# A routed expert layer on one core: two weighing pieces in front of the weights, two buffers of turned lists, a residual apart from its statistics, and last norms on VectorE

## Chip, core and metric

The kernel runs on 1 core of one Trainium2 chip. The metric is the device time of the whole program in microseconds; the median of three runs stands for a kernel.

## What is computed

Input x is 4 sequences of 1024 tokens with 128 features. The first half is a gated recurrence along the tokens, then a residual and a layer norm. The second half, on which the change works, sends every token to experts by product keys:

```python
xn = batch_norm(x)
q = (xn @ w_q.T).reshape(b, n, 2, h, kd).transpose(2, 0, 1, 3, 4)    # h = 8 heads
sim = einsum('pbnhd,hkpd->pbnhk', q, keys)                           # 32 keys a side
s, i = top_k(sim, 8)
all_scores = sx[..., :, None] + sy[..., None, :]
scores, pk = top_k(all_scores.reshape(b, n, h, 64), 8)
idx = take(ix * 32 + iy, pk)                                         # of 1024 experts
o = gelu(einsum('bnd,bnhkd->bnhk', x, key_in[idx])) * softmax(scores)
y = einsum('bnhk,bnhkd->bnd', o, key_out[idx])
out = layernorm(x + y)
```

## The kernel before

The tokens are worked in `NS = 16` steps m of 256 tokens; two steps make a chunk q of 512 (`NCH = 8`). The experts are not gathered. All 1024 inner products with `key_in` are made (`experts_in`, then `gelus`), the 64 chosen weights of each token are spread into a dense table p (`scatter`), the two tables are multiplied (`weigh`), and the product goes through `key_out` (`experts_out`).

Each engine has its own written order, and semaphores tie the orders together. For a step m the work passes:

- PE `scores`, ScalarE `sims_out`, VectorE `greatest` (8 largest of 32, L651) and `indices` (L659).
- GpSimd `candidate_sums` (last operation L265), ScalarE `exps` and `low_halves`, VectorE `top_sums` (L665).
- GpSimd `candidate_codes` (L270 to L281) and `over_eighth` (L287), ScalarE `signs` (L434).
- In the next step, VectorE `pack` (L672), `pick` (L684), then `sums_and_codes`: a copy of `exk` (L691), `codes` from `picked` and `masks` (L692), a sum and a reciprocal. GpSimd's `weights` (L292 to L301) and ScalarE's `convert` write `lists`. PE turns the lists, ScalarE copies them out of PSUM into `listsT` (`lists_out`, L444), and VectorE `hots_of` makes one-hot tables of each half of the lists (L708, L714, L718, twice in a step).
- PE `scatter` multiplies the one-hot tables, ScalarE `p_out` (L453) copies p into `pn`, and GpSimd `weigh` (L308) multiplies four pieces of 512 elements for each partition, `gl = pn * gl`, two steps later still.

GpSimd's order in a step m is `candidate_sums(m)`, `weights(m-1)`, `weigh(m-3)`, `candidate_codes(m)`, `over_eighth(m)`. VectorE's order is `greatest(m)`, `pack`, `pick` and `sums_and_codes` of m-1, `indices(m)`, `top_sums(m)`, `hots_of(m-1, 0)`, in odd steps from 5 on a `residual` with its `stats`, and `hots_of(m-1, 1)`. ScalarE runs `gelus` in steps 1, 2, 3, 5, 7, 9, 11 and 13, and `signs(m)` stands inside them, in front of the third piece.

The tail is written out by hand. Step 14's second half and step 15 go through `quarters` on PE, which keeps the two parts of each weight apart; ScalarE takes the low part (L531), and VectorE adds the high part and weighs (`both_parts`, L818 and L823). GpSimd weighs the first half of step 14 (L325). The last chunk is normed in two halves of 256 tokens.

Of the kernel before, what the change touches and what calls it, by code (L numbers as in the profile page):

```python
# [5 lines left out]
ALU = mybir.AluOpType  # L6
ACT = mybir.ActivationFunctionType
AX_X = mybir.AxisListType.X
F32 = mybir.dt.float32
F16 = mybir.dt.float16  # L10
# [4 lines left out]
P = 128  # L15
# [10 lines left out]
def seqffn_kernel(nc, x, w_in, w_select, w_gate, w_out, w_delta, log_a, gamma, beta, w_q, keys,  # L26
# [8 lines left out]
    NCH = T // CH  # L35
# [6 lines left out]
    NS = T // 2  # L42
# [11 lines left out]
    with ExitStack() as ctx:  # L54
        def sb(name, shape, dt=F32):
            return ctx.enter_context(nc.sbuf_tensor(name, shape, dt))
# [60 lines left out]
        masks = sb("masks", [P, 2, 1], U16)  # L117
        codes = sb("codes", [P, 2, 2 * SL], U16)
        lists = sb("lists", [P, 4, 2 * SL], F16)
        listsT = sb("listsT", [P, 2, 4, P // 2], F16)  # L120


        XW, YW = P * NI // 2, P * NJ // 2
# [9 lines left out]
        zf = nat[:, 0:CH, :]  # L133
        st2 = sb("st2", [P, CH, 6])
        mv2 = sb("mv2", [P, CH, 2])
        rstd2 = sb("rstd2", [P, CH])
# [49 lines left out]
        def wait(eng, name, value):  # L186
            if value <= 0:
                return
            eng.wait_ge(s[name], value)
# [33 lines left out]
        def _(pool):  # L223
# [27 lines left out]
            def candidate_sums(m):  # L251
                wait(pool, "vals_done", m * 2 + 2)
                wait(pool, "top_done", m)
                wait(pool, "dt_done", m)
                vx, vy = vals[:, 0], vals[:, 1]
                pool.tensor_tensor(cand[:, :, 0:8], vx[:, :, 0:1].to_broadcast([P, RH, 8]), vy, ALU.add)  # L256
                pool.tensor_tensor(cand[:, :, 8:12], vx[:, :, 1:2].to_broadcast([P, RH, 4]), vy[:, :, 0:4], ALU.add)
                pool.tensor_tensor(cand[:, :, 12:16].rearrange("p h (a b) -> p h a b", a=2),
                                   vx[:, :, 2:4].unsqueeze(3).to_broadcast([P, RH, 2, 2]),
                                   vy[:, :, 0:2].unsqueeze(2).to_broadcast([P, RH, 2, 2]), ALU.add)  # L260
                pool.tensor_tensor(cand[:, :, 16:20], vx[:, :, 4:8], vy[:, :, 0:1].to_broadcast([P, RH, 4]),
                                   ALU.add).then_inc(s["cand_done"], 1)
                wait(pool, "cand_done", m + 1)
                wait(pool, "ex_done", m)
                pool.tensor_tensor(dif[:, :, :], cand[:, :, :], cand[:, :, 0:1].to_broadcast([P, RH, NCAND]),  # L265
                                   ALU.subtract).then_inc(s["dif_done"], 1)
# [33 lines left out]
                wait(pool, "whi_done", m + 1)  # L300
                pool.tensor_tensor(lists[:, 3, :], flat, lists[:, 2, :], ALU.subtract).then_inc(s["wlo_done"], 1)  # L301

            def weigh(m):
                wait(pool, "p_evac", m * 2 + 2)
                wait(pool, "gelu_done", (m // 2 + 1) * JR)
                for r in range(4):
                    js = slice(4 * r, 4 * r + 4)
                    pool.tensor_tensor(gl[:, m % GL, js], pn[:, m % 3, js], gl[:, m % GL, js],  # L308
                                       ALU.mult).then_inc(s["a_done"], 1)

            for m in range(NS):
                candidate_sums(m)
                if m >= 1:
                    weights(m - 1)
                if m >= 3:
                    weigh(m - 3)
                candidate_codes(m)
                over_eighth(m)
            weigh(NS - 3)
            pool.wait_ge(s["hot_done"], 2 * NS)  # L320
            pool.wait_ge(s["p_evac"], LAST)
            for r in range(4):
                js = slice(4 * r, 4 * r + 4)
# [5 lines left out]
        def _(act):  # L329
# [110 lines left out]

            def lists_out(m):
                wait(act, "lists_mm", m + 1)
                wait(act, "hot_done", m * 2)
                act.activation(listsT[:, :, :, :].rearrange("p h f t -> p f h t"),  # L444
                               b_lists.rearrange("p (f h t) -> p f h t", f=4, h=2), ACT.Copy).then_inc(s["lists_evac"], 1)

            def p_out(m, hf):
# [31 lines left out]
            def spread2_half(u):  # L479
# [1 line left out]
                act.wait_ge(s["mv2_done"], NCH + u)  # L481
                act.wait_ge(s["out_done"], NCH - 1)
                act.activation(rstd2[:, n], mv2[:, n, 1], ACT.Sqrt, bias=eps[:, 0:1]).then_inc(s["sd2"], 1)

            def norm_out_half(u):
                act.wait_ge(s["nmr2_done"], NCH + u)
                act.wait_ge(s["stored"], 16 * (NCH - 1))
                for t in range(2 * u, 2 * u + 2):
                    end = act.activation(outb[:, t, :], zf[:, t, :], ACT.Identity, bias=nmr2[:, t:t + 1],
                                         scale=rstd2[:, t:t + 1])  # L490
                end.then_inc(s["out_done"], 1)

            normed(0)
            sims_out(0)
# [40 lines left out]
            norm_out(NCH - 2)  # L535
            for u in range(2):
                spread2_half(u)
                norm_out_half(u)

        @block.vector  # L540
        def _(dve):
# [158 lines left out]
            def hots_of(m, hf):  # L700
                at = slice(32 * hf, 32 * hf + 32)

                def spread(f, n):
                    v = listsT[:, hf, f, :].rearrange("p (g s) -> p g s", s=2)
                    return v.unsqueeze(2).to_broadcast([P, 32, n, 2])

                wait(dve, "lists_evac", m + 1)
                dve.tensor_tensor(hoty[:, at], iota[:, NI:].unsqueeze(1).to_broadcast([P, 32, NJ, 2]),  # L708
                                  spread(1, NJ), ALU.is_equal).then_inc(s["hoty_done"], 1)
                if m * 2 + hf == 2 * NS - 1:  # L710
                    dve.wait_ge(s["q_mm"], 2)
                else:
                    wait(dve, "p_mm", m * 2 - 1 + hf)
                dve.tensor_tensor(hotx[:, at], iota[:, 0:NI].unsqueeze(1).to_broadcast([P, 32, NI, 2]),  # L714
                                  spread(0, NI), ALU.is_equal)
                wait(dve, "hoty_done", m * 2 + hf + 1)
                both = listsT[:, hf, 2:4, :].rearrange("p w (g s) -> p (w g) s", s=2).unsqueeze(2)
                dve.tensor_tensor(hotw[:, :, at].rearrange("p w g j s -> p w (g j s)"),  # L718
                                  hoty[:, at].rearrange("p g j s -> p (g j s)").unsqueeze(1).to_broadcast(
                                      [P, 2, 32 * NJ * 2]),  # L720
                                  both.to_broadcast([P, 64, NJ, 2]), ALU.mult).then_inc(s["hot_done"], 1)
# [79 lines left out]
                    end = dve.bn_aggr(mv2[:, t, :], st2[:, t, :])  # L801
                end.then_inc(s["mv2_done"], 1)

            def last_scales(u):
                n = slice(2 * u, 2 * u + 2)
                dve.wait_ge(s["sd2"], NCH + u)
                dve.reciprocal(rstd2[:, n], rstd2[:, n]).then_inc(s["rstd2_done"], 1)
                dve.wait_ge(s["rstd2_done"], NCH + u)
                dve.scalar_tensor_tensor(out=nmr2[:, n], in0=mv2[:, n, 0], scalar=-1.0, in1=rstd2[:, n],
                                         op0=ALU.mult, op1=ALU.mult).then_inc(s["nmr2_done"], 1)  # L810

            def both_parts(h):
                m, hf = (LAST + h) // 2, (LAST + h) % 2
# [12 lines left out]
            dve.wait_ge(s["gelu_done"], NCH * JR)  # L826
            both_parts(0)
            residual(NCH - 2)
            stats(NCH - 2)
            both_parts(1)  # L830
            both_parts(2)
            scales(NCH - 2)
            for u in range(2):
                last_residual(u)
                last_scales(u)

        @block.tensor
        def _(pe):
# [215 lines left out]
```

## Time and profile before

| what | value |
|---|---|
| median of 3 runs | 490.32 us (487.49 to 490.91) |
| profiled execution, its own time | 490.44 us |
| its span, first to last instruction | 488.5 us |
| mean granted TensorE clock | 0.787 of full speed |
| busy: PE, VectorE, ScalarE, GpSimd | 359.3, 432.3, 245.4, 243.5 us |
| steps 1 to 15 begin on VectorE | 93 us to 428 us |
| last instruction of step 15's hot tables | ends 468.0 us |

Busy time of an engine is the union of its instructions' time. An idle time in square brackets stands before an instruction, with the engine and line that ended it. An instruction that waits inside the engine for a memory port shows no idle time: it shows a longer duration. So the durations of one line have to be compared over its repetitions.

### The profile page before, as it was taken

The page shows a single profiled execution, that of the slowest core. Times are in us where ns is not written, and L with a number is a line of the kernel's source. Part 1 is how long each engine was busy: PE and PEld are TensorE (multiplying, and loading weights), DVE is VectorE, ACT ScalarE, POOL GpSimd, SP SyncE. Part 2 cuts the span into 40 slices and gives each one's busy share as a digit, 9 for nine tenths or more (in the row PEclk, how much of TensorE's full clock was granted, in tenths as well). Part 3 has the DMA queues.
Part 4 walks back from the last instruction along what each step waited for, and adds up shares of the span by engine and source line. Part 5 has one row for each costly group of instructions (what it writes and reads, how often), then busy time and mean ns, then how long its engine had stood idle before and what let it go on. Part 6 is the DMA issues. An engine that isn't in the chain of part 4 may idle for free.

```text
span 488.5 us, 23430 instructions
## 1 busy us (share of the span) xinstructions
PE 359.3 (74%) x9713; PEld 266.5 (55%) x9713; DVE 432.3 (88%) x2701; ACT 245.4 (50%) x402; POOL 243.5 (50%) x341
## 2 busy tenths in 40 slices
PE   5979858137877778778777887687688778687565
PEld 3445544015545466447655674467356747487555
DVE  2458986999999869999999999989999999999993
ACT  2897664354555534364556445545464456242233
POOL 1023350453529461828382969262929483969030
PEclk9979956767595977797599768877797598867579
DMA  8900000000000000000000000000000000000001
GB/s 241 192 3 1 1 1 0 1 1 3 4 2 5 3 3 4 5 2 5 25 5 3 3 26 3 5 3 26 3 4 4 25 5 3 4 26 4 3 25 44
DMA packets 7658, 8.90 MB, mean 18 GB/s; under 512 B 896, under 2 KB 6912, under 8 KB 7424
## 3 DMA queue, kind: packets, MB, share of 16 engines
q1 hardware_dynamic: 6976, 7.34, 5.8%
q8 instruction: 76, 1.25, 1.1%
q14 instruction: 30, 0.25, 0.2%
q10 hardware_dynamic: 576, 0.07, 0.1%
HBM read 5.31 MB, written 2.10 MB: 15 GB/s over the span
## 4 chain that ended last, share of the span: by engine, by line
DVE 37%; PE 29%; issue 12%; POOL 5%; ACT 3%; DVEq 0%; ACTq 0%; POOLq 0%
PE psum L993 10%; DVE idx L659 7%; PE psum L946 7%; PE psum L980 6%; DVE vals L651 5%; DVE picked L684 5%; DVE arena L718 5%; DVE arena L714 4%; PE psum L926 4%; DVE arena L708 3%; POOL arena L308 2%; DVE top L665 2%; PE psum L918 1%; DVE words L672 1%; POOL code L278 1%
## 5 line engine op out<-in xcount | busy, mean ns | idle before, releaser
L946 PE MATMUL psum<-arena 64*64 64x16 f16 x7424 | 88.3, 182 | 61.0 <-issue 55.3
L946 PEld LDWEIGHTS psum<-arena 64*64 64x64 f16 x7424 | 81.2, 120 | 79.1 <-issue 73.6
L993 PE MATMUL psum<-ko,arena 64*128 64x128 f32 x1024 | 92.2, 358 | 1.9 <-issue 1.9
L993 PEld LDWEIGHTS psum<-ko,arena 64*128 64x128 f32 x1024 | 88.8, 269 | 2.9 <-issue 2.5
L659 DVE FIND_INDEX8 idx<-vals,sims 128x8 uint32<-128x32 f32 x512 | 82.6, 186 | 0.0
L714 DVE TENSOR_TENSOR arena<-iota,listsT 128x4096 f16<-128x4096 f16 x32 | 75.5, 2359 | 0.0
L980 PE MATMUL psum<-x1T,trn 128*64 128x256 f32 x512 | 65.6, 410 | 13.1 <-ACT arena L461 12.4
L308 POOL TENSOR_TENSOR arena<-arena 128x512 f32<-128x512 f32 x56 | 69.6, 1276 | 0.0
L980 PEld LDWEIGHTS psum<-x1T,trn 128*64 128x64 f32 x512 | 35.1, 146 | 49.7 <-ACT arena L461 25.4
L256 POOL TENSOR_TENSOR cand<-vals 128x128 f32<-128x128 f32 x16 | 9.4, 587 | 104.5 <-DVE vals L651 104.5
L453 ACT ACTIVATE arena<-psum 128x1024 f32<-128x1024 f32 x29 | 29.5, 1017 | 60.8 <-PE psum L946 60.8
L651 DVE MAX8 vals<-sims 128x8 f32<-128x32 f32 x512 | 49.0, 173 | 3.4 <-ACT sims L413 3.4
L926 PE MATMUL psum<-msim,xn 128*128 128x512 f32 x64 | 47.0, 875 | 1.2 <-ACT xn L405 1.2
L684 DVE MAX8 picked<-words 128x8 f32<-128x20 f32 x512 | 43.2, 164 | 5.0 <-ACT words L429 3.2
L461 ACT ACTIVATE arena<-psum 128x512 f32<-128x512 f32 x64 | 37.0, 595 | 13.3 <-PE psum L980 13.2
L718 DVE TENSOR_TENSOR arena<-arena,listsT 128x2048 f16<-128x2048 f16 x32 | 41.2, 1288 | 0.0
L659 DVE MATCH_VALUE_LOAD idx<-vals,sims 128x8 f32 x512 | 36.6, 72 | 0.0
L708 DVE TENSOR_TENSOR arena<-iota,listsT 128x1024 f16<-128x1024 f16 x32 | 26.1, 816 | 8.2 <-ACT listsT L444 8.2
L240 POOL TENSOR_TENSOR arena<-arena 128x512 f32<-128x512 f32 x8 | 10.3, 1286 | 45.4 <-ACT arena L370 45.4
L413 ACT ACTIVATE sims<-psum 128x512 f32<-128x512 f32 x32 | 19.0, 596 | 21.5 <-PE psum L926 21.2
L444 ACT ACTIVATE listsT<-psum 128x512 f16<-128x512 f16 x16 | 9.6, 597 | 37.4 <-PE psum L933 32.3
L862 PE MATMUL psum<-arena,trn 128*128 128x512 f32 x48 | 24.6, 652 | 1.7 <-ACT arena L373 1.7
(126 smaller groups left out, 570.2 us busy)
## 6 DMA issues: line engine op xcount, KB each, us to landing
x<-in_L_attn_x_dram SPq DMA_DIRECT2D x8, 256.0 KB, 5.6
out_dram<-nat SPq DMA_DIRECT2D x7, 256.0 KB, 2.5
ko<-in_L_ffn_key_out_dram SPq DMA_DIRECT2D x2, 512.0 KB, 9.9
nat<-in_L_ffn_key_in_dram SPq DMA_DIRECT2D x2, 256.0 KB, 10.1
nat<-in_L_ffn_keys_dram SPq DMA_DIRECT2D x2, 128.0 KB, 5.5
out_dram<-nat SPq DMA_DIRECT2D x2, 128.0 KB, 1.7
nat<-in_L_attn_W_delta_dram SPq DMA_DIRECT2D x1, 64.0 KB, 2.8
nat<-in_L_attn_W_in_dram SPq DMA_DIRECT2D x1, 64.0 KB, 2.7
```

Source lines behind the costliest of these rows:

```text
L308: pool.tensor_tensor(gl[:, m % GL, js], pn[:, m % 3, js], gl[:, m % GL, js], ALU.mult).then_inc(s["a_done"], 1)
L461: act.activation(gl[:, (2 * q) % GL:(2 * q) % GL + 2, 2 * r:2 * r + 2, :].rearrange("p m j w -> p j m w"), b_g[r % 2].rearrange("p (j m w) ...
L651: end = dve.max(vals[:, p, t * H + h, :], sims[:, m % 2, t, r, :])
L659: end = dve.max_index(idx[:, p, t * H + h, :], vals[:, p, t * H + h, :], sims[:, m % 2, t, r, :])
L684: end = dve.max(picked[:, w, r, :], words[:, w, r, :])
L708: dve.tensor_tensor(hoty[:, at], iota[:, NI:].unsqueeze(1).to_broadcast([P, 32, NJ, 2]), spread(1, NJ), ALU.is_equal).then_inc(s["hoty_don ...
L714: dve.tensor_tensor(hotx[:, at], iota[:, 0:NI].unsqueeze(1).to_broadcast([P, 32, NI, 2]), spread(0, NI), ALU.is_equal)
L718: dve.tensor_tensor(hotw[:, :, at].rearrange("p w g j s -> p w (g j s)"), hoty[:, at].rearrange("p g j s -> p (g j s)").unsqueeze(1).to_br ...
L926: pe.matmul(b_sim[t], xn[:, t], msim[:, :], start=True, stop=True).then_inc(s["sim_mm"], 1)
L946: end = pe.matmul(psum[64 * e:64 * e + 64, at:at + NJ], hotx[rows, g, :, e], hotw[rows, part, g, :, e], start=(part == 0), stop=(part == 1))
L980: end = pe.matmul(b_g[r % 2][64 * e:64 * e + 64, b * SW:(b + 1) * SW], trn[:, 9 + r, 64 * b:64 * b + 64], tokens[:, e], start=True, stop=True)
L993: end = pe.matmul(y2[:, e, m % 2] if m < NS - 1 else y_last[:, e], gl[rows, m % GL, j, :], ko[rows, j, :], start=(j == 0), stop=(j == NJ - 1))
```

## The change

- GpSimd: `weigh` takes a range of pieces. Pieces 0 and 1 of `weigh(m-3)` move ahead of `weights(m-1)`; pieces 2 and 3 stay behind it.
- `listsT` gets two buffers by the parity of m; `lists_out(m)` waits for the hot tables of step m-2 where it waited for those of m-1.
- GpSimd's last weighing (L325) waits for 31 of the 32 hot tables where it waited for all.
- Tail on VectorE: `residual` of chunk 6 (steps 12 and 13) stays ahead of `both_parts(1)`, and its `stats` move behind it.
- The last two half norms move from ScalarE (two activations with bias and scale) to VectorE (two subtract-and-multiply operations), and the small operation that made their bias goes.

```diff
+        listsT = sb("listsT", [P, 2, 2, 4, P // 2], F16)
...
+            def weigh(m, first=0, last=4):
                 wait(pool, "p_evac", m * 2 + 2)
                 wait(pool, "gelu_done", (m // 2 + 1) * JR)
+                for r in range(first, last):
...
             for m in range(NS):
                 candidate_sums(m)
+                if m >= 3:
+                    weigh(m - 3, 0, 2)
                 if m >= 1:
                     weights(m - 1)
                 if m >= 3:
-                    weigh(m - 3)
+                    weigh(m - 3, 2, 4)
                 candidate_codes(m)
                 over_eighth(m)
             weigh(NS - 3)
-            pool.wait_ge(s["hot_done"], 2 * NS)
+            pool.wait_ge(s["hot_done"], 2 * NS - 1)
...
             def lists_out(m):
                 wait(act, "lists_mm", m + 1)
-                wait(act, "hot_done", m * 2)
-                act.activation(listsT[:, :, :, :].rearrange("p h f t -> p f h t"),
+                wait(act, "hot_done", m * 2 - 2)
+                act.activation(listsT[:, m % 2].rearrange("p h f t -> p f h t"),
...
             for u in range(2):
                 spread2_half(u)
-                norm_out_half(u)
...
-            def last_scales(u):
+            def last_out(u):
                 n = slice(2 * u, 2 * u + 2)
                 dve.wait_ge(s["sd2"], NCH + u)
                 dve.reciprocal(rstd2[:, n], rstd2[:, n]).then_inc(s["rstd2_done"], 1)
                 dve.wait_ge(s["rstd2_done"], NCH + u)
-                dve.scalar_tensor_tensor(out=nmr2[:, n], in0=mv2[:, n, 0], scalar=-1.0, in1=rstd2[:, n],
-                                         op0=ALU.mult, op1=ALU.mult).then_inc(s["nmr2_done"], 1)
+                dve.wait_ge(s["stored"], 16 * (NCH - 1))
+                for t in range(2 * u, 2 * u + 2):
+                    end = dve.tensor_scalar(outb[:, t, :], zf[:, t, :], mv2[:, t:t + 1, 0], rstd2[:, t:t + 1],
+                                            ALU.subtract, ALU.mult)
+                end.then_inc(s["out_done"], 1)
...
             both_parts(0)
             residual(NCH - 2)
+            both_parts(1)
             stats(NCH - 2)
-            both_parts(1)
             both_parts(2)
             scales(NCH - 2)
             for u in range(2):
                 last_residual(u)
-                last_scales(u)
+                last_out(u)
```

## Rows read from the trace of the kernel before

**Rows 1.** The page's part 1: busy us, share of the span, instructions of each engine.

```profile
PE 359.3 (74%) x9713; PEld 266.5 (55%) x9713; DVE 432.3 (88%) x2701; ACT 245.4 (50%) x402; POOL 243.5 (50%) x341
```

**Rows 2.** The page's part 4: the chain that ended last, by engine.

```profile
DVE 37%; PE 29%; issue 12%; POOL 5%; ACT 3%; DVEq 0%; ACTq 0%; POOLq 0%
```

**Rows 3.** Timeline of GpSimd, step 8: start us, us, line, operation.

```profile
266.46 0.72 POOL L265 TENSOR_TENSOR dif<-cand 128x320 f32<-128x320 f32 x1
269.40 0.25 POOL L292 TENSOR_SCALAR zscaled<-zinv 128x16 f32<-128x16 f32 x1 [2.22 <-DVE zinv L698]
...
271.03 4.96 POOL L308 TENSOR_TENSOR arena<-arena 128x512 f32<-128x512 f32 x4
275.93 0.76 POOL L270 CAST iyf<-idx 128x128 f32<-128x128 uint32 x1
...
284.70 0.75 POOL L287 TENSOR_TENSOR above<-cand,top 128x320 f32<-128x320 f32 x1
```

**Rows 4.** Timeline of VectorE, the same step 8.

```profile
268.20 0.31 DVE L691 COPY exk<-picked 128x256 uint16<-128x256 uint16 x1
268.41 0.42 DVE L692 TENSOR_TENSOR codes<-picked,masks 128x256 uint16<-128x256 uint16 x1
...
275.61 0.93 DVE L708 TENSOR_TENSOR arena<-iota,listsT 128x1024 f16<-128x1024 f16 x1
```

**Rows 5.** Timeline after step 15: GpSimd's weigh of step 13, VectorE beside it.

```profile
447.93 5.19 POOL L308 TENSOR_TENSOR arena<-arena 128x512 f32<-128x512 f32 x4
...
448.56 1.03 DVE L672 SCALAR_TENSOR_TENSOR words<-sgn,code 128x320 uint16<-128x320 f32 x1 [0.56 <-issue]
...
452.50 0.78 DVE L691 COPY exk<-picked 128x256 uint16<-128x256 uint16 x1
```

**Rows 6.** One line's instructions: duration ns min/median/max, first and last start us.

```profile
L672 DVE SCALAR_TENSOR_TENSOR words<-sgn,code x16: 492/497/1034, 96.1 to 448.6; 128x320 uint16<-128x320 f32 x16
...
L708 DVE TENSOR_TENSOR arena<-iota,listsT x32: 658/754/1248, 106.9 to 464.0; 128x1024 f16<-128x1024 f16 x32
```

**Rows 7.** Timeline, step 1: GpSimd's L287 between two hot tables of VectorE.

```profile
110.09 1.73 POOL L287 TENSOR_TENSOR above<-cand,top 128x320 f32<-128x320 f32 x1
...
111.13 1.23 DVE L708 TENSOR_TENSOR arena<-iota,listsT 128x1024 f16<-128x1024 f16 x1
```

**Rows 8.** VectorE idle: timeline of steps 4 and 10, then the waits (us, times, longest).

```profile
167.86 1.39 DVE L684 MAX8 picked<-words 128x8 f32<-128x20 f32 x16 [1.89 <-ACT words L429]
180.88 0.69 DVE L708 TENSOR_TENSOR arena<-iota,listsT 128x1024 f16<-128x1024 f16 x1 [4.00 <-ACT listsT L444]
...
324.39 0.69 DVE L708 TENSOR_TENSOR arena<-iota,listsT 128x1024 f16<-128x1024 f16 x1 [2.02 <-ACT listsT L444]
...
DVE arena L708 <- ACT listsT L444: 8.2, 5, 4.0
DVE picked L684 <- ACT words L429: 3.2, 3, 1.9
```

**Rows 9.** Timeline of ScalarE, step 3, inside the gelus.

```profile
161.99 0.47 ACT L434 ACTIVATE sgn<-above 128x320 f32<-128x320 f32 x1 [0.86 <-POOL above L287]
```

**Rows 10.** Timeline of the tail, VectorE, GpSimd and PE.

```profile
459.73 0.69 DVE L708 TENSOR_TENSOR arena<-iota,listsT 128x1024 f16<-128x1024 f16 x1 [0.72 <-ACT listsT L444]
...
468.06 3.75 POOL L325 TENSOR_TENSOR arena<-arena 128x256 f32<-128x256 f32 x4 [14.94 <-DVE arena L718]
...
471.18 0.87 DVE L733 BATCH_NORM_STATS2 st<-nat 128x6 f32<-128x128 f32 x4
472.09 0.38 DVE L737 BATCH_NORM_AGGREGATE mv<-st 128x2 f32<-128x6 f32 x4
...
473.10 1.04 PE L970 MATMUL psum<-arena 64*64 64x32 f16 x64 [2.57 <-DVE arena L818]
```

**Rows 11.** Timeline: a norm on VectorE in the first half, the last norm on ScalarE.

```profile
67.04 2.14 DVE L617 TENSOR_SCALAR x<-x,mv,rstd 128x128 f32<-128x128 f32 x8
...
485.52 0.88 ACT L489 ACTIVATE nat<-nat,nmr,rstd 128x128 f32<-128x128 f32 x2 [0.43 <-DVE nmr L809]
```

More of the change, by code:

```diff
@@ L119, in seqffn_kernel @@
         lists = sb("lists", [P, 4, 2 * SL], F16)
-        listsT = sb("listsT", [P, 2, 4, P // 2], F16)
+        listsT = sb("listsT", [P, 2, 2, 4, P // 2], F16)
         XW, YW = P * NI // 2, P * NJ // 2
@@ L301, in weights @@
                 pool.tensor_tensor(lists[:, 3, :], flat, lists[:, 2, :], ALU.subtract).then_inc(s["wlo_done"], 1)
-            def weigh(m):
+            def weigh(m, first=0, last=4):
                 wait(pool, "p_evac", m * 2 + 2)
                 wait(pool, "gelu_done", (m // 2 + 1) * JR)
-                for r in range(4):
+                for r in range(first, last):
                     js = slice(4 * r, 4 * r + 4)
@@ L483, in spread2_half @@
                 act.activation(rstd2[:, n], mv2[:, n, 1], ACT.Sqrt, bias=eps[:, 0:1]).then_inc(s["sd2"], 1)
[L485 to L491, printed above, removed]
             normed(0)
@@ L703, in spread @@
                 def spread(f, n):
-                    v = listsT[:, hf, f, :].rearrange("p (g s) -> p g s", s=2)
+                    v = listsT[:, m % 2, hf, f, :].rearrange("p (g s) -> p g s", s=2)
                     return v.unsqueeze(2).to_broadcast([P, 32, n, 2])
@@ L716, in hots_of @@
                 wait(dve, "hoty_done", m * 2 + hf + 1)
-                both = listsT[:, hf, 2:4, :].rearrange("p w (g s) -> p (w g) s", s=2).unsqueeze(2)
+                both = listsT[:, m % 2, hf, 2:4, :].rearrange("p w (g s) -> p (w g) s", s=2).unsqueeze(2)
                 dve.tensor_tensor(hotw[:, :, at].rearrange("p w g j s -> p w (g j s)"),
```

## The prediction

> **What bounds the kernel now.** I read the busy shares first: VectorE is busy for 432.3 of 488.5 us, and no other engine for more than 74% [rows 1]. The chain of waits says the same less sharply, with VectorE at 37%, PE at 29% and GpSimd at 5% [rows 2]. Then I took VectorE's idle times by what ended them. Between steps 1 and 15 there are few: 8.2 us ahead of the hot tables (L708), 0.72 of it in the tail, and 3.2 us in the middle of `pick` (L684) [rows 8, 10]. So in the steps VectorE sets the pace, and PE is the second limit: where L708 waits 4.00 us in step 4 and 2.02 us in step 10, the lists were ready and PE came to turn them late. Whatever makes VectorE's own instructions longer is paid in nearly every step; whatever makes GpSimd faster is paid back only where somebody waits for it.
>
> The next thing to read is not idle time but duration. VectorE and GpSimd hold each other up inside their instructions. L672 takes 0.49 us in the steps and 1.03 us once, at 448.56, while GpSimd weighs; L691, elsewhere 0.31 us, takes 0.78 us at 452.50, and ends just after the fourth weighing piece [rows 4 to 6]. In step 1 GpSimd's L287 waits for a hot table to end and then holds the next, L708, to 1.23 us against its 0.68: 0.55 us for an instruction that takes 0.75 undisturbed [rows 3, 6, 7]. The two engines take turns: a GpSimd instruction that asks while a VectorE one holds goes next, ahead of VectorE's following one.
>
> **Two pieces ahead of the weights, steps 3 to 15.** Step 8 stands for all. GpSimd ends L265 at 267.18 and then idles 2.22 us until the reciprocal is there at 269.4 [rows 3]. Two pieces of 4.96 / 4 = 1.24 us fit almost: 267.13 to 269.6. On GpSimd that delays the weights by 0.2 us at most, and the turned lists came in front of their use by over 1 us in such steps, so that costs nothing. It starts the codes as soon as the indices are done, 1.3 us ahead of the hot tables and 1.6 us earlier than now.
>
> But in those 2.22 us VectorE runs L691 (from 268.20) and L692 (from 268.41) [rows 4]. Today GpSimd is idle there and four pieces run beside the index searches, which show no delay. After the change piece 0 lets go at about 268.3: L691 loses 0.0 to 0.1. Piece 1 is ready at 268.35, before L692 starts, and takes its turn when L691 lets go, at about 268.5. L692 then waits for the whole piece. No row shows L692 beside GpSimd, nor a whole 512-element piece ahead of a VectorE instruction, so this is bounded. Below: 0, if L692 gets in first or does not mind; then piece 1 runs on beside the index searches. Above: L287 held for its 0.75 less 0.2 us, so a piece holds for 1.24 less 0.2, or 1.05. By elements, 0.55 x 512 / 320 = 0.88. Below zero is excluded, since nothing of VectorE's is removed there. I take 1.05: L692 reads two tiles in SBUF like L708 and L672, which both were held, and the order of requests favours the piece.
>
> The Trainium skill, "SBUF — State Buffer", section "Who interferes with whom", speaks against this edit: an instruction of VectorE with two SBUF inputs and one of GpSimd that reads SBUF exclude each other for the whole instruction, in order of issue. Rows 5 and 7 agree, with 0.54 and 0.55 us. "GPSIMD Engine Reference", section "Instruction dispatch", puts two inputs at 2.5 cycles an element; at its 1.2 GHz that would be an estimate of 1.07 us a piece, and the sum would be the same within 0.2 us.
>
> How often is it paid? In ten steps in full (3, 5, 7 to 11, 13 to 15). In step 4 the wait in `pick` of 1.89 us [rows 8] moves L691 behind both pieces: nothing. In steps 6 and 12 smaller waits of the same kind leave about 0.35 each. Sum 10 x 1.05 + 0.7 = 11.2 us. Some of it falls into idle time that VectorE has anyway, since PE came late there: 1.05 of step 3 in the 5.9 us of step 4; 2.0 of steps 9 and 10 in the 2.02 of step 10; and steps 6 and 12 share the rest of the two waits (8.2 - 4.0 - 2.0 - 0.7 and 3.2 - 1.9, or 2.8 us), which takes 1.4 of steps 5 and 6 and 0.8 of steps 11 and 12 [rows 8]. Absorbed 5.2, left +6.0 us.
>
> **What the earlier codes give.** In step 8 the tail of weighing no longer holds L708 (0.93 against 0.68, so 0.25 [rows 4, 6]), and three code instructions fewer take turns at 0.09 each: 0.5 gained. But `over_eighth` (L287), which now ends behind the hot tables at 285.4 [rows 3], falls between them as in step 1, at 0.55. Net 0, from -0.1 to +0.1 a step. L287 is earlier by some 4 us, and ScalarE's signs with it. VectorE does not wait for the signs in the steps. They hold up the gelus only 0.86 us in step 3 [rows 9], and by as much in steps 7 and 13, where VectorE has no idle time after them to give back. Step 3's gives -0.9, through PE, in step 4.
>
> **The tail.** (a) `weigh(13)` starts earlier and meets L718 and L672 where it met L672 and L691; against that L672's idle 0.56 goes [rows 5]. L718 and L672 lose about 1.0 and 0.8, before 0.53, 0.47 and 0.56: with L287's 0.55, net +0.4, taken between -0.5 and +1.5. (b) With two buffers `lists_out(15)` no longer waits for the hot tables of step 14, and L708's 0.72 goes [rows 10]; next is VectorE itself, so -0.7. In the steps this buffer changes nothing. (c) L325's four pieces, 3.75 us with one VectorE instruction of 1.2 in between, hence 0.63 each holding 0.44, now begin beside `scales` and the last hot table and hold up four VectorE instructions: up to 4 x 0.44; I take +1.4. Its results were not awaited before 474, so earlier is no gain. (d) The chain ends over L818 of `both_parts(1)`, for which PE waits 2.57 us, then 9.3 us of `experts_out`. Statistics of 0.87 + 0.38 go behind it: -1.25. What is late next is `both_parts(2)`, which stays where it was and was ahead of the second `experts_out` by just about this, so the gain may end at 1.0. (e) The last norm: 0.88 us and a hop on ScalarE plus 0.16 for the bias become two instructions at 2.14 / 8 = 0.27 on VectorE [rows 11], about 0.45 less. The new wait for `stored` has only the last half's residual queued behind it, and PE is later. Tail: +0.4 - 0.7 + 1.4 - 1.25 - 0.45 = -0.6.
>
> **Sum.** +6.0 - 0.9 + 0 - 0.6 = +4.5 on the profiled execution's 490.44 (span 488.5, 1.9 outside it), which is 0.1 above the median: 495 us. With 0.88 a piece it is +3; with nothing absorbed +10.
>
> **Rivals.** *Slower: L692 held by piece 1*, the forecast: from the point at which a held L692 costs more than 0.2 us a step it decides over everything else. For it: rows 5 and 7. Against: L691 lets go and piece 1 asks within 0.1 us of each other.
> *No collision*: L692 goes first, or is not held. Then the steps give 0.1 x 12 of L691 less 0.9, and the tail -0.6: 490. The page's rule on the order of issue would give this too if L692 were the earlier one.
> *Faster: the earlier signs free PE and ScalarE.* The chain of waits runs in step 3 over weighing, codes and L287 into the gelus. If the 5.9 us of step 4 and the 2.0 of step 10 go with it, without a collision, and L325 holds nothing: 490.4 - 7.9 - 2.0 = 480.5; half of that is 485. Against: ScalarE waits for L287 only 0.86 us there, and the rest of PE's lateness is its own.
> *The buffer does nothing, the tail grows*: L325's four turns cost 1.8 and the statistics give 1.0, without collision: 491.
>
> **How the numbers follow.** Collision 0.62, no collision 0.20, faster 0.12, tail 0.06. A measurement of this kernel can tell about 1% (4.9 us) from no change. The collision's 495 lies at that bound, 495.2, and its upper side is the longer one: 0.6 of it above. Slower by over 1%: 0.62 x 0.6 and little else, 0.38; within 1%: 0.25 + 0.20 + 0.06, less 0.01: 0.49; faster: 0.13. The range runs from 486 (half of the faster rival cut off) to 500 (most of the collisions unabsorbed). The likeliest case's own range is 492 to 500.
>
> **What the profile after would show.** L692 at 1.3 to 1.5 us in steps without an idle time in `pick`, against 0.42 everywhere now; L691 at 0.31 to 0.4; L708 at 0.76 and L287 at 1.73 as in step 1; no idle time ahead of step 15's L708; L325 from about 463 us at 4 to 6 us; PE's wait for L818 about 1.2 us shorter; the last L617-like pair at 0.6 us. The prediction is wrong if L692 stays at 0.42, or if the 4.00 us of step 4 go.

## The result and the profile after

The changed kernel takes 494.92 us (median of 5 runs, 491.66 to 496.38) against 490.32 (median of 5 runs, 486.33 to 490.91): a ratio of 1.012, with a 95% interval of 1.0076 to 1.0163. The ratio is formed from all the runs of both kernels; the two medians alone give 1.009. The change makes the kernel slower by about 1%: less than 2%, but clear of the noise, since of these ten runs every one of the changed kernel is slower than every one of before. Its profiled execution was the lowest of its runs, 491.66 us with a span of 489.9, so it is only 1.4 us longer than the span of before; the parts below are read from it, the size of the loss from the medians.

The page after, parts 1 and 4 (to be held against [rows 1, 2]):

```profile
PE 355.5 (73%) x9713; PEld 261.3 (53%) x9713; DVE 447.8 (91%) x2703; ACT 244.8 (50%) x398; POOL 238.7 (49%) x341
...
DVE 54%; PE 18%; issue 11%; ACT 4%; POOL 0%; DVEq 0%; ACTq 0%
```

VectorE is busy 15.5 us longer with two more instructions, and the chain runs more over VectorE (54% against 37%) and less over PE (18% against 29%). The kernel after has other line numbers: L684 is the copy L691 of before, L685 the codes L692, L665 `pack`, L701, L707 and L711 the hot tables L708, L714 and L718, L327 the last weighing L325.

VectorE and GpSimd after, timelines of step 7, and all instructions of L685 (duration ns min/median/max); [rows 3, 4] show step 8 of before:

```profile
240.18 0.40 DVE L684 COPY exk<-picked 128x256 uint16<-128x256 uint16 x1
240.48 1.49 DVE L685 TENSOR_TENSOR codes<-picked,masks 128x256 uint16<-128x256 uint16 x1
241.89 0.27 DVE L689 TENSOR_REDUCE zsum<-exk 128x16 f32<-128x128 f32 x1
...
238.45 0.72 POOL L265 TENSOR_TENSOR dif<-cand 128x320 f32<-128x320 f32 x1
239.13 2.56 POOL L308 TENSOR_TENSOR arena<-arena 128x512 f32<-128x512 f32 x2
242.54 0.25 POOL L292 TENSOR_SCALAR zscaled<-zinv 128x16 f32<-128x16 f32 x1 [0.85 <-DVE zinv L691]
...
251.97 1.73 POOL L287 TENSOR_TENSOR above<-cand,top 128x320 f32<-128x320 f32 x1
...
L685 DVE TENSOR_TENSOR codes<-picked,masks x16: 411/1486/1496, 98.4 to 455.2; 128x256 uint16<-128x256 uint16 x16
```

An instruction is called held by the time by which it takes longer than undisturbed. L684 is held 0.1 us by the end of the first piece, and L685 starts beside the second piece and takes 1.49 us where it took 0.42: 1.07 us lost, with no idle time to show it. The two pieces took 2.56 instead of 2.48 us, because L684 had its turn between them. In 12 of the 13 steps it is so. In step 12 L684 comes while the second piece is running, takes the whole wait (1.44 us) and L685 none. One more thing changes in the steps: L287 takes 1.73 us in 11 of the 13 steps, where it took 0.75 in 11 of before. VectorE's instructions behind L711 in step 7, and those of step 8 with GpSimd's L287:

```profile
253.02 0.68 DVE L719 TENSOR_TENSOR nat<-psum,x 128x512 f32<-128x512 f32 x1
...
278.26 0.51 DVE L737 SCALAR_TENSOR_TENSOR nmr<-mv,rstd 128x4 f32<-128x4 f32 x1
...
277.02 1.73 POOL L287 TENSOR_TENSOR above<-cand,top 128x320 f32<-128x320 f32 x1
```

L287 waits for the end of L711, and that is most of its 1.73 us. VectorE pays little for it: in odd steps the residual L719 comes next and is not held (0.68 us, as in the steps of before), and in even steps from 6 on L737 is held 0.34 us (0.51 against 0.16).

Step by step, from one `pack` to the next, VectorE now needs 25.04 us for odd steps and 23.8 for even ones, against 24.00 and 22.67. Over steps 3 to 15 L684 and L685 are 14.7 us longer (12 steps at 0.07 + 1.07, one at 1.12). What paid most of it back in this execution is idle time: between the `pack` of step 1 and that of step 15 VectorE was idle 11.2 us before (0.56 of it just ahead of the last `pack`) and 1.2 us after. Of the 4.00 us ahead of step 4's hot table [rows 8] this is left, and it is the only idle time in the steps:

```profile
177.01 0.74 DVE L701 TENSOR_TENSOR arena<-iota,listsT 128x1024 f16<-128x1024 f16 x1 [1.19 <-ACT listsT L446]
```

In sum: 1.3 us less in the first half, where nothing was changed; 329.95 to 334.27 us between the two `pack`s, or +4.3; and from the last `pack` to the end 40.0 to 38.3, or -1.7. A part of the +4.3 belongs to the tail's work: between the `pack`s of steps 14 and 15 the change is +1.7, of which L684 and L685 are 1.1.

The end of step 15 after, VectorE and GpSimd (to be held against [rows 5]):

```profile
445.42 2.83 DVE L707 TENSOR_TENSOR arena<-iota,listsT 128x4096 f16<-128x4096 f16 x1
448.18 2.29 DVE L711 TENSOR_TENSOR arena<-arena,listsT 128x2048 f16<-128x2048 f16 x1
...
451.58 0.50 DVE L665 SCALAR_TENSOR_TENSOR words<-sgn,code 128x320 uint16<-128x320 f32 x1
...
444.91 1.20 POOL L287 TENSOR_TENSOR above<-cand,top 128x320 f32<-128x320 f32 x1
446.06 8.33 POOL L308 TENSOR_TENSOR arena<-arena 128x512 f32<-128x512 f32 x4
```

Here `weigh(13)` meets the hot tables: L707 is held 0.55 us by L287 and L711 1.07 us by a piece, and the four pieces take 8.33 us because the tables hold them. L665 and L684, which the pieces held before, are free: L665 starts at 451.58, just as the second piece ends (451.61), has its turn ahead of the third, and that piece takes 1.60 us instead of 1.26; L684 starts behind the fourth.

The tail after (to be held against [rows 10, 11]):

```profile
465.07 0.69 DVE L737 SCALAR_TENSOR_TENSOR nmr<-mv,rstd 128x4 f32<-128x4 f32 x1
...
466.30 2.81 DVE L707 TENSOR_TENSOR arena<-iota,listsT 128x4096 f16<-128x4096 f16 x1
469.03 1.74 DVE L711 TENSOR_TENSOR arena<-arena,listsT 128x2048 f16<-128x2048 f16 x1
...
481.90 0.42 DVE L786 TENSOR_TENSOR nat<-psum,x 128x256 f32<-128x256 f32 x1 [1.72 <-ACT nat L477]
...
484.13 0.60 DVE L804 TENSOR_SCALAR nat<-nat,mv,rstd 128x128 f32<-128x128 f32 x2 [0.47 <-DMA out_dram<-nat]
485.33 0.42 DVE L786 TENSOR_TENSOR nat<-psum,x 128x256 f32<-128x256 f32 x1 [0.60 <-PE psum L989]
...
465.03 6.32 POOL L327 TENSOR_TENSOR arena<-arena 128x256 f32<-128x256 f32 x4 [10.64 <-DVE arena L711]
```

L327 holds three instructions of VectorE by 0.53, 0.53 and 0.52 us (0.16, 2.28 and 1.22 us undisturbed). The idle 0.72 us ahead of step 15's hot table is gone. The first half's residual now waits for ScalarE's norm of chunk 6, no longer for PE; the second half's waits for PE, 0.60 us.

### The profile page after: what moved, and what is told of

Same layout as the page of the kernel before. It is cut to its first block, busy times and chain, and to the rows that moved or that the text cites. A ratio compares the mean times of both kernels' runs of the same rounds, so it can differ in the third digit from the quotient of the medians.

```text
span 489.9 us, 23440 instructions
## 1 busy us (share of the span) xinstructions
PE 355.5 (73%) x9713; PEld 261.3 (53%) x9713; DVE 447.8 (91%) x2703; ACT 244.8 (50%) x398; POOL 238.7 (49%) x341
## 3 DMA queue, kind: packets, MB, share of 16 engines
q8 instruction: 76, 1.25, 1.0%
## 4 chain that ended last, share of the span: by engine, by line
DVE 54%; PE 18%; issue 11%; ACT 4%; POOL 0%; DVEq 0%; ACTq 0%
DVE idx L652 12%; DVE vals L644 7%; DVE picked L677 7%; DVE arena L711 6%; PE psum L976 6%; DVE arena L707 5%; PE psum L942 4%; PE psum L922 3%; DVE arena L701 3%; PE psum L989 3%; DVE codes L685 3%; DVE top L658 3%; DVE exk L684 1%; DVE words L665 1%; ACT L463 1%
## 5 line engine op out<-in xcount | busy, mean ns | idle before, releaser
L942 PE MATMUL psum<-arena 64*64 64x16 f16 x7424 | 86.2, 181 | 61.9 <-issue 53.6
L942 PEld LDWEIGHTS psum<-arena 64*64 64x64 f16 x7424 | 79.2, 118 | 79.3 <-issue 73.7
L989 PE MATMUL psum<-ko,arena 64*128 64x128 f32 x1024 | 89.6, 351 | 4.1 <-issue 4.1
L989 PEld LDWEIGHTS psum<-ko,arena 64*128 64x128 f32 x1024 | 86.2, 262 | 5.0 <-issue 4.7
L707 DVE TENSOR_TENSOR arena<-iota,listsT 128x4096 f16<-128x4096 f16 x32 | 75.6, 2364 | 0.0
L308 POOL TENSOR_TENSOR arena<-arena 128x512 f32<-128x512 f32 x56 | 73.9, 1342 | 0.0
L976 PEld LDWEIGHTS psum<-x1T,trn 128*64 128x64 f32 x512 | 35.2, 148 | 49.6 <-ACT arena L463 23.8
L922 PE MATMUL psum<-msim,xn 128*128 128x512 f32 x64 | 49.3, 914 | 1.2 <-ACT xn L407 1.2
L711 DVE TENSOR_TENSOR arena<-arena,listsT 128x2048 f16<-128x2048 f16 x32 | 42.0, 1313 | 0.0
L240 POOL TENSOR_TENSOR arena<-arena 128x512 f32<-128x512 f32 x8 | 10.3, 1286 | 44.4 <-ACT arena L372 44.4
L281 POOL TENSOR_TENSOR code<-ixf,iyf 128x64 f32<-128x64 f32 x16 | 31.7, 1979 | 0.0
L415 ACT ACTIVATE sims<-psum 128x512 f32<-128x512 f32 x32 | 19.0, 596 | 23.8 <-PE psum L922 23.8
L929 PE MATMUL psum<-ident,lists 128*128 128x128 f16 x64 | 7.0, 240 | 28.0 <-POOL lists L301 16.3
L431 ACT ACTIVATE words<-words 128x320 uint16<-128x320 uint16 x16 | 9.0, 564 | 34.1 <-DVE words L665 33.9
```

The costliest lines, as they stand in the source:

```text
L281: pool.tensor_tensor(code[:, :, 16:20], ixf[:, :, 4:8], iy[:, :, 0:1].to_broadcast([P, RH, 4]), ALU.add).then_inc(s["code_done"], 1)
L922: pe.matmul(b_sim[t], xn[:, t], msim[:, :], start=True, stop=True).then_inc(s["sim_mm"], 1)
L942: end = pe.matmul(psum[64 * e:64 * e + 64, at:at + NJ], hotx[rows, g, :, e], hotw[rows, part, g, :, e], start=(part == 0), stop=(part == 1))
L976: end = pe.matmul(b_g[r % 2][64 * e:64 * e + 64, b * SW:(b + 1) * SW], trn[:, 9 + r, 64 * b:64 * b + 64], tokens[:, e], start=True, stop=True)
L989: end = pe.matmul(y2[:, e, m % 2] if m < NS - 1 else y_last[:, e], gl[rows, m % GL, j, :], ko[rows, j, :], start=(j == 0), stop=(j == NJ - 1))
```

## Experiments

Lines that are the same in two kernels are the same code; "the tail" is the time from the last `pack` to the end of the span. Every kernel has one profile. In the seven profiles with the changed kernel's tail code (its own and those of e2, e3, e4, e8, e9 and e10) the tail takes from 37.6 to 38.7 us, so a difference below 1 us between two tails counts only where the instruction that makes it can be named. The kernel before was run on the same chip beside each, and its median moved between 490.1 and 492.1 us, so kernels are compared by their ratios to it. Steps and idle time are read as above.

**e1, only the split.** The kernel before with the two pieces moved and nothing else:

```diff
                 candidate_sums(m)
+                if m >= 3:
+                    weigh(m - 3, 0, 2)
                 if m >= 1:
                     weights(m - 1)
                 if m >= 3:
-                    weigh(m - 3)
+                    weigh(m - 3, 2, 4)
```

> The kernel before with only the two pieces moved ahead of the weights. Theory (L692 is held by the second piece): L692 at 1.45 to 1.5 us in about 12 steps, the steps at 25.0 (odd) and 23.8 us (even), and the time 3 to 7 us above before: 494 to 497. Rival (the loss comes from the tail or the other edits): L692 may still be long, but the time is that of before within 1.5 us.

495.28 us, ratio 1.0102 (1.006 to 1.0144). All instructions of the codes operation, here L694:

```profile
L694 DVE TENSOR_TENSOR codes<-picked,masks x16: 414/1486/1496, 99.2 to 458.8; 128x256 uint16<-128x256 uint16 x16
```

The split alone makes the loss and its signature, and the steps are the same 25.04 and 23.8 us. Idle time in the steps was 4.5 us here, not 1.2, and from the `pack` of step 1 to that of step 15 this profile has 337.1 us, 7.2 more than before: the same steps cost this execution 2.8 us more than the profiled one of the change.

**e2, all but the split.** The changed kernel with `weigh(m - 3, 0, 4)` behind the weights.

> The changed kernel with all four pieces behind the weights again. Theory: L692 back at 0.42 us, the steps as before with the 4 us idle time in step 4, the tail of the changed kernel; net 0 to 3 us below before: 487.5 to 490.5. Rival (the loss comes from the other edits): 493 to 496.

488.55 us, ratio 0.9971 (0.994 to 1.0002); the codes operation is at 0.42 us throughout, and 11.6 us are idle in the steps. The other edits together gain 0 to 3 us. The rival falls.

**e3, one piece in front.**

```diff
                 if m >= 3:
-                    weigh(m - 3, 0, 2)
+                    weigh(m - 3, 0, 1)
...
-                    weigh(m - 3, 2, 4)
+                    weigh(m - 3, 1, 4)
```

> The changed kernel with one piece ahead of the weights and three behind. Theory: the piece ends at the moment L691 asks, so L691 at 0.35 to 0.4 and L692 at 0.42 us; codes still begin at the end of the index searches. VectorE gets 1.06 us back in 12 or 13 steps, and PE's lateness takes some of it: 483 to 488. Rival (the split costs by something other than the second piece's turn, as the later weights or more turns in the hot tables): 492 to 495.

486.54 us, ratio 0.9922 (0.989 to 0.9953): faster than both kernels. Timeline of VectorE, step 7:

```profile
240.78 0.38 DVE L684 COPY exk<-picked 128x256 uint16<-128x256 uint16 x1
241.07 0.41 DVE L685 TENSOR_TENSOR codes<-picked,masks 128x256 uint16<-128x256 uint16 x1
```

The first piece costs 0.07 us; the second was the whole loss. The steps take 23.93 and 22.9 us. The codes still start at the end of the index searches, but L287 is not where it was: it takes 0.75 us in 10 of the 13 steps here. That is not what gave the time back, since VectorE pays no less for it: nothing in odd steps, and 0.57 us in step 14, where it holds a hot table (L701, 1.25 us), against 0.34 in the change. As expected, part of what VectorE got back turned into idle time: there are 9.6 us of it.

**e4, codes from one input.** L685 reads `picked` and `masks`; here it is two operations of half the size with a constant:

```diff
-                dve.tensor_tensor(codes[:, :, :], picked16[:, 0, :, 1].unsqueeze(1).to_broadcast([P, 2, 2 * SL]),
-                                  masks[:, :, :].to_broadcast([P, 2, 2 * SL]), ALU.bitwise_and).then_inc(
+                dve.tensor_scalar(codes[:, 0, :], picked16[:, 0, :, 1], NE - NJ, None, ALU.bitwise_and)
+                dve.tensor_scalar(codes[:, 1, :], picked16[:, 0, :, 1], NJ - 1, None, ALU.bitwise_and).then_inc(
```

> The changed kernel, two pieces in front; L692 with its two inputs in SBUF becomes two operations of half the size with one input and a constant. Theory, if only instructions with two SBUF inputs (and the copy L691) are held: each of the two stays at 0.2 to 0.3 us, and the time is 484 to 489. Rival (whatever VectorE issues second is held by the piece): the first of the two takes about 1.3 us and the time stays at 493 to 496.

493.95 us, ratio 1.0088 (1.0058 to 1.0118). My theory missed here and the rival held:

```profile
241.52 0.38 DVE L684 COPY exk<-picked 128x256 uint16<-128x256 uint16 x1
241.81 1.29 DVE L685 TENSOR_SCALAR codes<-picked 128x128 uint16<-128x128 uint16 x1
243.02 0.21 DVE L686 TENSOR_SCALAR codes<-picked 128x128 uint16<-128x128 uint16 x1
```

The first of the two is held 1.07 us, the same as the two-input form. One input does not keep an operation out of the conflict. (In step 4 it was the copy, at 1.12 us, that was held.) The Trainium skill, "VectorE: DVE Perf Modes", section "Mode 2×_2P — use both read ports for one tensor", names the forms with one source and a destination in SBUF that read over both ports; the copy and this operation are of those forms. No run here shows which mode they were in.

**e8, the copy and the codes exchanged**, two pieces in front:

```diff
-                dve.tensor_copy(exk16, picked16[:, :, :, 0]).then_inc(s["exk_done"], 1)
                 dve.tensor_tensor(codes[:, :, :], picked16[:, 0, :, 1].unsqueeze(1).to_broadcast([P, 2, 2 * SL]),
...
+                dve.tensor_copy(exk16, picked16[:, :, :, 0]).then_inc(s["exk_done"], 1)
```

> The changed kernel, two pieces in front, with the codes operation ahead of the exk copy. Theory (GpSimd's second piece takes its turn after whichever instruction comes first): the codes operation at 0.45 to 0.5 us, the exk copy, now second, at 1.2 to 1.4 us. Rival (the codes operation is slow by itself beside weighing, or the copy is never held for a whole piece): codes still above 1 us, or both short.

499.39 us in one run, so only its durations are read. Timeline of VectorE, step 7, the codes now L684 and the copy L687:

```profile
244.44 0.48 DVE L684 TENSOR_TENSOR codes<-picked,masks 128x256 uint16<-128x256 uint16 x1
244.84 1.38 DVE L687 COPY exk<-picked 128x256 uint16<-128x256 uint16 x1
```

In 9 of the 13 steps the copy, which now comes second, is held for the whole piece, 1.07 us. So it is a matter of turns: piece, VectorE's first, piece, VectorE's second. The exact moment decides: in steps 4, 6, 10 and 12 the second piece was already running when the first of the two came, which was held (0.78, 1.47, 1.51 and 1.12 us), and the copy stayed at 0.30.

**e9, three pieces in front** (`weigh(m - 3, 0, 3)` and `(3, 4)`).

> The changed kernel with three pieces in front and one behind. Theory (only L684 and L685 can be held there, and each instruction of VectorE is held by at most one turn): L685 stays at 1.48 us, the third piece runs beside the sum, the reciprocal and the index searches and holds none of them (0.28, 0.25 and 0.18 us); the weights come some 0.6 us later, which nobody waits for; time 492 to 496 as the change. Rival (the cost grows with the weighing in front): another 1 us a step, 500 to 508.

497.64 us, ratio 1.0163 (1.008 to 1.0245). All instructions of two of VectorE's lines, then GpSimd in step 8:

```profile
L685 DVE TENSOR_TENSOR codes<-picked,masks x16: 414/1486/1499, 99.4 to 460.7; 128x256 uint16<-128x256 uint16 x16
...
L689 DVE TENSOR_REDUCE zsum<-exk x16: 272/274/280, 99.8 to 461.0; 128x16 f32<-128x128 f32 x16
...
268.01 3.97 POOL L308 TENSOR_TENSOR arena<-arena 128x512 f32<-128x512 f32 x3
```

The third piece runs beside the sum and the searches and holds none of them; it takes 1.46 us itself, as it waits for the end of L685; the steps are at 25.04 and 23.8 us as with two. The time is 1.6 us above the range that was expected and 2.4 below the rival's. Its interval, from four runs, overlaps that of the change. Whether the weights, 0.6 us later, cost something stays open; in two steps that wait for ScalarE (4 and 6) the copy lost 0.3 and 0.6 us on top of L685's 1.07.

**e10, half pieces.** The two pieces in front are cut into four instructions of 256 elements.

```diff
-                for r in range(first, last):
-                    js = slice(4 * r, 4 * r + 4)
-                    pool.tensor_tensor(gl[:, m % GL, js], pn[:, m % 3, js], gl[:, m % GL, js],
-                                       ALU.mult).then_inc(s["a_done"], 1)
+                size = 2 if last == 2 else 4
+                for r in range(4 * first, 4 * last, size):
+                    js = slice(r, r + size)
+                    end = pool.tensor_tensor(gl[:, m % GL, js], pn[:, m % 3, js], gl[:, m % GL, js], ALU.mult)
+                    if (r + size) % 4 == 0:
+                        end.then_inc(s["a_done"], 1)
```

> The changed kernel, the two pieces in front cut into four instructions of 256 elements, the same signals. Theory (VectorE's instruction is held for one turn, and the turn is as long as the GpSimd instruction): L685 at 0.95 instead of 1.48 us, steps 0.5 us shorter, 488 to 492. Rival (held until the weighing is over, or a fixed price): L685 stays at 1.3 us or more and the time at 493 to 496.

492.39 us, ratio 1.004 (0.9999 to 1.008), 0.4 us above the range that was expected. Timeline of VectorE, step 8, the copy now L686 and the codes L687:

```profile
269.61 0.53 DVE L686 COPY exk<-picked 128x256 uint16<-128x256 uint16 x1
270.04 0.94 DVE L687 TENSOR_TENSOR codes<-picked,masks 128x256 uint16<-128x256 uint16 x1
```

Half the length, half the wait: L687 is held 0.53 us. The copy loses 0.2 instead of 0.1, as a turn ends later. Steps without idle time are at 24.63 and 23.38 us, 0.4 below the change. The profiled execution was the longest of the ten (496.38 us), so nothing else is read from it.

**The tail, on top of e3.** e5 lets GpSimd's last weighing wait for all hot tables again:

```diff
-            pool.wait_ge(s["hot_done"], 2 * NS - 1)
+            pool.wait_ge(s["hot_done"], 2 * NS)
```

> One piece in front, and GpSimd's last weighing waits for all 32 hot tables again. Theory (its four pieces hold up VectorE's small scale operation and the last hot tables by 0.53 us three times): these three instructions back at 0.16, 2.28 and 1.22 us, the tail 1 to 1.6 us shorter than with one piece in front alone, 484.5 to 486 at the same place. Rival (earlier results of that weighing let PE start earlier, which pays for it): no change or longer, 486 to 488.

486.41 us, ratio 0.9912 (0.9878 to 0.9945), which cannot be told from e3's. The time lies in the rival's range, but the kernel before was 2 us slower beside it than beside e3, so the times decide nothing. The tail of the profile can be told apart: 36.9 us against 38.7. VectorE, then GpSimd:

```profile
458.44 0.16 DVE L737 SCALAR_TENSOR_TENSOR nmr<-mv,rstd 128x4 f32<-128x4 f32 x1
...
459.12 2.28 DVE L707 TENSOR_TENSOR arena<-iota,listsT 128x4096 f16<-128x4096 f16 x1
461.32 1.22 DVE L711 TENSOR_TENSOR arena<-arena,listsT 128x2048 f16<-128x2048 f16 x1
...
462.62 3.75 POOL L327 TENSOR_TENSOR arena<-arena 128x256 f32<-128x256 f32 x4 [14.12 <-DVE arena L711]
```

All three holds are gone, 1.6 us together, and the trace shows nobody waiting for the later weighing. The rest of the 1.8 us is a wait of VectorE for ScalarE ahead of the residual of chunk 6, 0.52 us in e3 and 0.22 here.

e6 puts `stats(NCH - 2)` ahead of `both_parts(1)` again.

> One piece in front, and the statistics of chunk 6 ahead of the second half's sums again. Theory: PE's last quarter comes 1.25 us later, and the end is 1.0 to 1.25 us later: about 487.5. Rival (the norm of chunk 6, which the last residual waits for, sets the end anyway): within 0.3 us of one piece in front alone.

487.88 us, ratio 0.9962 (0.9925 to 0.9998). Its tail takes 39.5 us, 0.8 longer than e3's. But e3's tail holds its own wait of 0.52 us for ScalarE, which neither e6 nor e7 has; against e7's tail, 38.1 us, e6's is 1.4 longer. The 1.0 to 1.25 that were expected lie between, and the rival (within 0.3) falls.

e7 restores the last two norms on ScalarE.

> One piece in front, and the last two half norms on ScalarE again. Theory: 0.45 us later at the end (0.88 + 0.16 us and a hop in place of 0.6 us). Rival (the new wait for the stored chunk ahead of the last residual costs as much as the move gives): no change in the profile's tail.

489.35 us, ratio 0.9926 (0.9884 to 0.9968), not to be told from e3. VectorE's two last residuals and the norm between them, first in e3, then in e7 (where the residual is L795 and the norm on ScalarE):

```profile
477.48 0.42 DVE L786 TENSOR_TENSOR nat<-psum,x 128x256 f32<-128x256 f32 x1 [1.72 <-ACT nat L477]
479.70 0.60 DVE L804 TENSOR_SCALAR nat<-nat,mv,rstd 128x128 f32<-128x128 f32 x2 [0.46 <-DMA out_dram<-nat]
480.21 0.42 DVE L786 TENSOR_TENSOR nat<-psum,x 128x256 f32<-128x256 f32 x1
...
480.52 0.43 DVE L795 TENSOR_TENSOR nat<-psum,x 128x256 f32<-128x256 f32 x1 [1.72 <-ACT nat L477]
482.80 0.42 DVE L795 TENSOR_TENSOR nat<-psum,x 128x256 f32<-128x256 f32 x1 [0.33 <-PE psum L995]
```

From the second residual to the end of the span e7 has 5.0 us and e3 4.5 (before 5.0, after 4.5), which is what the move gives. But in e3 the second residual stands behind the first half's norm on VectorE, which waits 0.46 us for the stored chunk, and it comes 2.73 us after the first; in e7 it comes after 2.28. From the first residual to the end both have 7.28 us: here the rival holds, and the move gives nothing. It counts where PE is late for the second residual anyway: from the first residual to the end e1, with the norms on ScalarE, has 8.42 us and the changed kernel 7.96. The steps of e7 are the code of e3, and VectorE was idle 14.0 us in them against 9.6: that much moves between two executions.

e11 is e5 with ScalarE's wait as with one buffer, `wait(act, "hot_done", m * 2)`.

> One piece in front, GpSimd's last weighing behind all 32 hot tables, and ScalarE's copy of the turned lists waiting as with one buffer. Theory: the idle 0.72 us ahead of step 15's first hot table comes back and the tail is 0.7 us longer than in the run without this; nothing in the steps. Rival (the buffer also freed something in the steps): idle time ahead of the hot tables grows in the steps too.

486.97 us, ratio 0.9942 (0.99 to 0.9984). Timeline of VectorE:

```profile
454.45 0.69 DVE L701 TENSOR_TENSOR arena<-iota,listsT 128x1024 f16<-128x1024 f16 x1 [0.72 <-ACT listsT L446]
```

The idle 0.72 us is back, and the tail is 37.4 us against 36.9; e5's had 0.22 us of waiting for ScalarE that this one has not, so the buffer's share is 0.5 to 0.7. In the steps it frees nothing: ScalarE's copy of the turned lists waits for PE in 14 steps and for VectorE's hot tables once, in the tail, as in the kernel before.

## Why the prediction was right

The time, 494.92 us, is 0.1 from the 495 that was given, and the mechanism that was named decided it. That it came so close is luck in good part, as the second point shows. By its steps:

- **L692 held by the second piece: right, and its price too.** 1.05 us was taken, between 0 and 1.05; every run with a full second piece shows 1.07, and e3, e8 and e10 tell the turn apart from all else. L691's 0 to 0.1 is 0.07 in most steps.
- **How often, and what is absorbed: both too small.** 11.2 us were counted. 14.7 came in the profile: the waits in `pick` that were to shield steps 4, 6 and 12 had gone, so these paid in full, and a step costs 1.14 us with L684's 0.07, not 1.05. Absorbed and gained were to be 5.2 + 0.9; the idle time fell by 10.0 us. The two errors cancel in part: without the tail's work the steps came out at +3.8 against +5.1 in the changed kernel's profile. With the tail's -1.2 against -0.6 the parts give +2.6 on the profiled execution where +4.5 was told. The two profiled executions differ by only 1.2 us, since the unchanged first half gave 1.3; the medians differ by 4.6, since the changed kernel's profiled execution is 3.3 us below its median. In e1's profile the same steps cost 2.8 us more, with 4.5 us idle left instead of 1.2. Executions of one kernel lie 5 us apart, so the sum's size is borne out by the medians, and the agreement to 0.1 us is luck.
- **The 4.00 us of step 4: the forecast's own sign of being wrong came in the main.** "The prediction is wrong if ... the 4.00 us of step 4 go" stands there, and 1.19 us were left, and nothing of the 1.89 in `pick`. The step shortened from 27.77 us to 24.15. ScalarE's signs waited for L287 there for 0.86 us before and 0.69 in e2, and not at all in any kernel with a piece in front. The rest goes with PE: with one piece in front and the same code the step takes 24.88, 25.06 and 25.44 us at a mean granted TensorE clock of 0.84 of full speed in it (e5, e3, e6), 26.58 at 0.80 (e7) and 26.81 at 0.74 (e11). Near 0.80 stand the kernel before with 27.77 (0.81), e2 with 27.13 (0.79), e7 with 26.58 and e1 with 25.85. So the -0.9 for the signs is of the right size, 0.5 to 1.2 us between e7 and those two, and the changed kernel's 0.84 is the luck of its execution. That the lower clock makes the step longer is argued from these rows and was not tested by itself.
- **What the earlier codes give: the net right, its terms not.** L287 is at 1.73 us, as told, but it costs VectorE 0 or 0.34 us a step, not 0.55: what comes next on VectorE is not a hot table. The gain was put at 0.5 and is smaller too (the first hot table, 0.92 to 0.75 us, and less than 0.1 lost on the following ones). Against the 1.14 us of L684 and L685 the odd steps are 1.04 us longer and the even ones 1.12, so the net is -0.1 to 0.
- **Tail, (a) `weigh(13)`: right mechanism, wrong sign.** The holds on L707 and L711 are 0.55 and 1.07 us and `pack` got 0.56 of idle back; the prediction then let L672 lose 0.8 more. But L672 (now L665) came just as a piece ended and took its turn ahead of the next, and L684 came behind the last. Between the `pack`s it costs 0.5, behind them it gives 0.53 + 0.47: net -0.5 instead of +0.4.
- **(b) two buffers: right.** The idle 0.72 went; e11 shows 0.5 to 0.7 of it at the end. **(c) L325 ahead of the last hot table: right, its hold too small.** +1.4 was taken from 0.44 a hold; three holds of 0.53 are 1.6, and e5 gets 1.8 back with a wait of another cause. The fourth piece met an instruction that it does not hold. **(d) statistics behind the sums: right.** 1.25, at least 1.0, was taken; e6 shows 0.8 against e3 and 1.4 against e7, and 1.1 is what the other terms leave of the changed kernel's -1.7. PE's wait for L814 is 1.68 us, 0.9 shorter where 1.2 was told. What came next was ScalarE's norm of chunk 6, for which the residual waits 1.72 us: the prediction looked for the next limit in `both_parts(2)` only. **(e) the norm: right for this kernel.** 0.45 was taken and 0.46 measured (e1 against the change), because PE was late for the second residual, as the prediction said. Where PE is not late the wait for the stored chunk takes it all back (e7).
- **The rivals.** e2 excludes that the tail or the buffer made the loss. "No collision" is e3 in all but the missing piece, at 486.5, not the 490 that was worked out, since the tail and the idle time gave more. The faster rival's idle time did go, with the collision beside it. (The chances of "within 1%" add up to 0.50, where 0.49 is written; nothing hangs on it.)

## What to carry to other kernels

When GpSimd's work is moved into an idle slot, look at what VectorE runs in that slot, not only at how long the slot is: the price of a meeting here was one whole GpSimd instruction less about 0.2 us, paid by VectorE's next instruction of the kinds named below, and it appeared as a longer duration and not as idle time. One piece that ends as VectorE asks was free: e3 is 0.8% faster than before, of which the other edits are 0.3% (e2, itself not to be told from none). The piece after it was the whole loss. If it has to lie there, it can be cut: half the length halved the wait of the codes (0.53 for 1.07), at 0.1 us more on the copy. And an instruction that takes longer than it did need not cost anybody that time: L287 went from 0.75 to 1.73 us, and VectorE paid 0 or 0.34 for it.

## What the runs showed of the hardware

- GpSimd and VectorE took strict turns where they met: in e9 L685 waits for the second piece (1.49 us for 0.42), and the third piece for L685 (1.46 us for 1.24). Holding times: 0.53 us for 256 elements and two inputs (of 0.72), 1.07 for 512 (of 1.24), 0.55 for L287's 320 with one broadcast input (of 0.75).
- Held by it were two-input operations in SBUF, a 16-bit copy with step 2, and a 16-bit operation with a constant (e4, not expected). Not held were `TENSOR_REDUCE` (0.27 us beside a piece in e9), the index searches, the statistics (L726, 0.27 to 0.28 us each beside a piece in the changed kernel), and operations with one input in PSUM and one in SBUF (L814 at 1.27 us, L719 at 0.68).
- Executions of one kernel lie up to 7 us apart (e5: 483.16 to 489.97 in 12 runs), and the idle time of VectorE in the steps differs by 4.4 us between profiles of the same steps (e3 and e7). Most of it is waiting for turned lists, for which ScalarE had waited for PE; 2.1 us in e3 and 4.2 in e7 are waiting inside `pick` for ScalarE itself (L431). With eleven runs of e3 a gain of 0.8% was clear; the 0.3% of e2 was not, in twelve. Parts of that size need the durations in the profile, not the medians.
